# Attention denominators, row maxima and expert tokens turned as 32x32 squares on the vector engine instead of on the matrix engine

## The reference

```
xn  = layernorm(x)
q, k, v = xn @ Wq, xn @ Wk, xn @ Wv          # 16 heads of 64
attn = softmax(q @ k.T / 8)                   # per head, 2048 x 2048
a   = concat(attn @ v) @ Wo + bo
e   = argmax_e(xn @ router_w[e])              # 8 experts, one per token
f   = square(relu(xn @ expert_fc[e])) @ expert_proj[e].T
out = x + a + f
```

## Time and profile before

| | us |
|---|---|
| runs of the kernel | 1388.52 median of 3 (1387.92 to 1388.96) |
| the profiled execution, its own time | 1389.63 |
| its span, first to last instruction | 1387.9 |
| PE busy | 1365.8 (98% of the span) |
| POOL busy | 1121.8 (81%) |
| DVE busy | 1078.0 (78%) |
| ACT busy | 735.2 (53%) |
| the 16 DMA engines, the kernel's own transfers | 20.8% of their span |
| mean granted TensorE clock | 0.993 of full speed |

### The profile page before, as it was taken

One profiled execution on the slowest core, in us unless ns is written; L12 is line 12 of the kernel. 1 busy time (PEld: TensorE's weight loads), 2 busy tenths in 40 slices (PEclk: granted clock), 3 DMA queues, 4 the chain that ended last, 5 costly groups with the idle time before them and its releaser, 6 DMA issues.

```text
span 1387.9 us, 20006 instructions
## 1 busy us (share of the span) xinstructions
PE 1365.8 (98%) x6447; PEld 866.1 (62%) x6447; DVE 1078.0 (78%) x1468; ACT 735.2 (53%) x1316; POOL 1121.8 (81%) x908
## 2 busy tenths in 40 slices
PE   7899999999999999999999999999999999999997
PEld 4566666566665666666766666656667666656644
DVE  7987887786787767777777777778677777788877
ACT  4465455565464554554644645545546446556543
POOL 7779997777787877877878877879777788789995
PEclk8999999999999999999999999999999999999998
DMA  4241113220132201331113311123112231111000
GB/s 104 58 120 41 37 41 70 70 67 20 43 89 57 60 19 43 94 69 44 34 39 84 73 40 43 43 71 90 24 42 55 64 79 26 24 23 33 11 19 23
DMA packets 65255, 72.38 MB, mean 52 GB/s; under 512 B 9024, under 2 KB 38272, under 8 KB 65152
## 3 DMA queue, kind: packets, MB, share of 16 engines
q1 hardware_dynamic: 64128, 69.01, 20.3%
q0 software_dynamic: 1024, 2.10, 0.5%
HBM read 17.83 MB, written 5.11 MB: 17 GB/s over the span
## 4 chain that ended last, share of the span: by engine, by line
PE 93%; DVE 2%; POOL 1%; DMA 1%; issue 1%; SPq 1%; ACT 1%; POOLq 0%; DVEq 0%; ACTq 0%
PE OB L1116 31%; PE SB L1062 17%; PE SB L1069 16%; PE MB L1088 15%; PE XB L1153 2%; PE XB L1144 2%; PE XB L1162 2%; PE XB L1050 1%; PE XB L1043 1%; POOL acc L505 1%; DVE mx L767 1%; PE XB L1123 1%; PE XB L1125 1%; PE XB L1124 1%; DMA K<-low 1%
## 5 line engine op out<-in xcount | busy, mean ns | idle before, releaser
L505 POOL TENSOR_TENSOR acc<-acc,ex 128x512 f32<-128x512 f32 x717 | 915.9, 1304 | 99.9 <-DVE acc L790 40.4
L767 DVE TENSOR_REDUCE mx<-MB 128x1 f32<-128x512 f32 x992 | 655.9, 688 | 228.9 <-PE MB L1088 224.1
L619 ACT ACTIVATE ex<-SB 128x512 f32<-128x512 f32 x1024 | 607.2, 599 | 329.8 <-PE SB L1069 262.0
L1116 PE MATMUL OB<-ex,V 128*64 128x512 f32 x2048 | 452.7, 594 | 0.0
L1062 PE MATMUL SB<-Q,K 128*128 128x512 f32 x1024 | 421.9, 412 | 0.5 <-ACT ex L619 0.5
L1069 PE MATMUL SB<-Q,K 128*128 128x512 f32 x1024 | 399.8, 390 | 0.8 <-DMA Q<-mrow 0.8
L1088 PE MATMUL MB<-K,Q 128*128 128x512 f32 x992 | 389.1, 392 | 1.6 <-DVE mx L773 0.6
L1116 PEld LDWEIGHTS OB<-ex,V 128*64 128x64 f32 x2048 | 143.9, 137 | 284.3 <-issue 273.0
L1062 PEld LDWEIGHTS SB<-Q,K 128*128 128x128 f32 x1024 | 192.6, 188 | 96.5 <-issue 53.5
L790 DVE TENSOR_TENSOR acc<-acc,ex 128x512 f32<-128x512 f32 x179 | 205.0, 1145 | 13.5 <-ACT ex L619 1.0
L1088 PEld LDWEIGHTS MB<-K,Q 128*128 128x128 f32 x992 | 186.1, 188 | 46.7 <-DVE mx L767 5.0
(11 more groups left out here) (136 smaller groups left out, 608.8 us busy)
## 6 DMA issues: line engine op xcount, KB each, us to landing
Q<-high SPq DMA_DIRECT2D x124, 128.0 KB, 2.3
K<-high SPq DMA_DIRECT2D x112, 128.0 KB, 2.3
Q<-low SPq DMA_DIRECT2D x64, 128.0 KB, 2.4
K<-low SPq DMA_DIRECT2D x56, 128.0 KB, 2.3
w<-fc SPq DMA_DIRECT2D x23, 256.0 KB, 2.7
w<-projT SPq DMA_DIRECT2D x23, 256.0 KB, 3.1
sorted_x<-res SPq DMA_DIRECT2D x1, 1472.0 KB, 6.9
tok<-sorted_x SPq DMA_DIRECT2D x23, 64.0 KB, 1.7
```

The costliest lines, as they stand in the source:

```text
L505: pool.tensor_tensor(a[:, :], src[:, :], EX[h][ex_slot(kt)][:, :], ALU.add).then_inc(done, 1)
L619: act.activation(EX[h][ex_slot(kt)][:, :], SB[bank_of(n, 2 * kt + h)][:, :], ACT.Exp).then_inc(a_e[h], 1)
L767: dve.tensor_reduce(mx[:, m % 2, u:u + 1], MB[bank_of(m, i)][:, :], AX.X, ALU.max).then_inc(v_m, 1)
L1116: mm = pe.matmul(OB[own[h], :], V[(n // JB) % 2][:, k, own[h]], EX[h][ex_slot(k)][:, :], start=(k == 0), stop=(k == NT - 1))
```

## The change

It takes the three turns away from PE and gives them to DVE, whose transpose turns each 32x32 square of a tile by itself.

- **Denominators.** `denominators`, `take_sums` and `invert` are gone. At kt 0 of block n DVE runs `fold_sums(n - 1)`: for each head it transposes `acc` (128x512) into `rd` in squares and reduces the squares' rows, which leaves 16 columns; together a 128x32 tile `part`, in which the four groups of 32 partitions are still to be added. `sum_parts` does this in one small operation a step: kt 1 a copy of 64x32, kt 2 an add of 64x32, kt 3 a copy of 32x32, kt 4 an add of 32x32, kt 5 the reciprocal of 32x32, kt 6 a transpose of 32x32 into `row`. SP writes `row` to DRAM (`store_row`), waits for it, and reads it back spread over 64 partitions for each head (`spread_rd`) into `rd`. POOL's `normalise` stays at kt 10 and waits for these transfers.
- **Maxima.** `nm` has 32 columns, of which 8 are used; `turn_max` is four DVE transposes of 32x32 at kt 12 straight into `mrow`. The matmul and ACT's copy are gone.
- **Tokens.** The tile is read in four transfers that put the 32x32 squares in each other's place, and one DVE transpose of 128x128 at kt 3 finishes the turn. The matmul and ACT's copy are gone.

The last block's denominators are still made on PE.

```
-AT_DEN, AT_KV, AT_Q, AT_WO, AT_NM, AT_T = 8, (1, 9), 5, 13, 11, 12
-AT_INV, AT_ON = 8, 10
+AT_KV, AT_Q, AT_WO, AT_NM, AT_T = (1, 9), 5, 13, 11, 12
+AT_FOLD, AT_ON = 0, 10
...
+        turned = rd
+        spare = halves[:, :, :].rearrange("p t s -> p (t s)")
+        part, upper, half = (spare[0:r, k * SQ:(k + 1) * SQ] for k, r in enumerate((P, 2 * SQ, 2 * SQ)))
+        third, den, inv, row = (sb(n_, [SQ, SQ]) for n_ in ("third", "den", "inv", "row"))
+        rows_rd = nc.dram_tensor("rows_rd", (2, QB), F32, kind="Internal").ap()
...
+                def store_row(n):
+                    wait(sp, v_row, n.times(1, 1))
+                    wait(sp, d_rd, n.times(32))
+                    sp.dma_start(rows_rd.rearrange("h (t b) -> (h t) b", b=SQ), row[:, :]).then_inc(d_row, 16)
+
+                def spread_rd(n):
+                    wait(sp, d_row, n.times(16, 16))
+                    for h in range(2):
+                        sp.dma_start(rd[own[h], :], rows_rd[h:h + 1, :].to_broadcast([DH, QB])).then_inc(d_rd, 16)
...
                 def normalise(n):
-                    wait(pool, v_rd, n.times(2, 2))
-
+                    wait(pool, d_rd, n.times(32, 32))
                     wait(pool, a_o, n.times(1, 1))
...
+                def turn_max(m):
+                    wait(dve, v_nm, m.times(1, 1))
...
+                    for j in range(P // SQ):
+                        squares = slice(j * SQ, (j + 1) * SQ)
+                        ins = dve.transpose(mrow[:, squares].bitcast(F32), nm[squares, :].bitcast(F32))
+                    ins.then_inc(v_mrow, 1)
...
+                def turn_tokens(r):
+                    wait(dve, d_tile, r.times(TD, TD))
+                    wait(dve, t_up, r.times(1))
+                    dve.transpose(tokT[:, :], tok[:, :]).then_inc(v_tok, 1)
...
+                def fold_sums(n):
+                    for h in range(2):
+                        wait(dve, sums[h][n % 2], added(n, NT - 1))
+                        if h == 0:
+                            wait(dve, g_on, n.times(1))
+                        else:
+                            wait(dve, v_part, n.times(2, 1))
+                        dve.transpose(turned[:, :], acc[h][n % 2][:, :]).then_inc(v_turn, 1)
+                        wait(dve, v_turn, n.times(2, h + 1))
+                        dve.tensor_reduce(part[:, h * QB // SQ:(h + 1) * QB // SQ], turned[:, :].rearrange("p (t k) -> p t k", k=SQ),
+                                          AX.X, ALU.add).then_inc(v_part, 1)
+
+                def sum_parts(n, kt):
+                    if kt == 1:
+                        wait(dve, v_part, n.times(2, 2))
+                        dve.tensor_copy(upper[:, :], part[2 * SQ:4 * SQ, :]).then_inc(v_upper, 1)
+                    if kt == 2:
...
+                        dve.tensor_tensor(half[:, :], part[0:2 * SQ, :], upper[:, :], ALU.add).then_inc(v_sum2, 1)
...
+                    if kt == 6:
+                        wait(dve, v_inv, n.times(1, 1))
+                        wait(dve, d_row, n.times(16))
+                        dve.transpose(row[:, :], inv[:, :]).then_inc(v_row, 1)
```

More of the change, by code:

```diff
@@ L646, in kv @@
                                        ACT.Copy).then_inc(a_v, 1)
-                def max_rows(m):
-                    wait(act, t_nm, m.times(1, 1))
-                    if not (m.i is None and m.off == 0):
-                        old = m - 1
-                        wait(act, d_nm[old % QS], (old // QS).times(32, 32))
-                    act.activation(mrow[:, :], XB[0:2 * TB, 0:P], ACT.Copy).then_inc(a_nm, 1)
                 def take_o(n):
@@ L693, in high_q0 @@
                     ins.then_inc(a_q, 1)
-                def copy_tokens(r):
-                    wait(act, t_tok, r.times(1, 1))
-                    act.activation(tokT[:, :], XB[:, 0:P], ACT.Copy).then_inc(a_tok, 1)
                 def rectify(r):
@@ L753, in one @@
                             high_q(m)
-                        if kt == AT_DEN and not (n.i is None and n.off == 0):
-                            take_sums(n - 1)
-                        if kt == AT_T and before(n, NB - 1):
-                            max_rows(n + 1)
                 schedule(act, first, one, lambda: take_o(Lin(NB - 1)))
@@ L777, in minus_max @@
                     wait(dve, v_m, m.times(UNITS, UNITS))
-                    wait(dve, t_nm, m.times(1, -1))
-                    dve.tensor_reduce(nm[:, m % 2, :], mx[:, m % 2, :].rearrange("p (a b) -> p a b", b=JB), AX.X,
+                    if m.off == 0:
+                        dve.wait_ge(g_i, 6)
+                    dve.tensor_reduce(nm[:, 0:2 * TB], mx[:, m % 2, :].rearrange("p (a b) -> p a b", b=JB), AX.X,
                                       ALU.max, negate=True).then_inc(v_nm, 1)
+                def turn_max(m):
+                    wait(dve, v_nm, m.times(1, 1))
+                    if not (m.i is None and m.off == 0):
+                        old = m - 1
+                        wait(dve, d_nm[old % QS], (old // QS).times(MD, MD))
+                    for j in range(P // SQ):
+                        squares = slice(j * SQ, (j + 1) * SQ)
+                        ins = dve.transpose(mrow[:, squares].bitcast(F32), nm[squares, :].bitcast(F32))
+                    ins.then_inc(v_mrow, 1)
                 def add(n, kt):
@@ L936, in first @@
                         maxima(Lin(1), u)
+                        if u == 0:
+                            turn_max(Lin(0))
                     choose()
@@ L948, in one @@
                             minus_max(n + 1)
+                        if kt == AT_T and before(n, NB - 1):
+                            turn_max(n + 1)
                         if kt in AT_KV and before(n, NB - JB):
@@ L959, in one @@
                         add_own(n, kt)
-                        if kt == AT_INV and not start:
-                            invert(n - 1, 0)
-                            invert(n - 1, 1)
+                        if kt == AT_FOLD and not start:
+                            fold_sums(n - 1)
+                        if not start:
+                            sum_parts(n - 1, kt)
                         for part in AT_PLACE.get((n.off, kt), ()):
@@ L1146, in make_kv @@
                         mm.then_inc(t_v, 1)
-                def denominators(n):
-                    take_spare(a_den, n.times(1, 1))
-                    for h in range(2):
-                        wait(pe, sums[h][n % 2], added(n, NT - 1))
-                    for h in range(2):
-                        mm = pe.matmul(XB[own[h], :], ones[:, 0:DH], acc[h][n % 2][:, :], start=True, stop=True)
-                    mm.then_inc(t_den, 1)
                 def project(n):
@@ L1164, in project @@
                     mm.then_inc(t_wo, 1)
-                def turn_max(m):
-                    take_spare(a_nm, m.times(1, 1))
-                    wait(pe, v_nm, m.times(1, 1))
-                    pe.transpose(XB[0:2 * TB, 0:P], nm[:, m % 2, :], ident[:, :]).then_inc(t_nm, 1)
                 def first():
@@ L1206, in first @@
                             logits(c)
-                    for u in range(EARLY):
-                        max_unit(Lin(1), u)
-                    turn_max(Lin(0))
-                    for u in range(EARLY, MIDDLE):
+                    for u in range(MIDDLE):
                         max_unit(Lin(1), u)
@@ L1238, in one @@
                             project(n - 1)
-                        if kt == AT_T and before(n, NB - 1):
-                            turn_max(n + 1)
-                        if kt == AT_DEN and not start:
-                            denominators(n - 1)
                         for m, tile, tiles in batches(n, kt):
```

74 lines of the change are left out of this document (40 added, 34 removed).

## The result

The changed kernel takes **1466.61 us** (median of 4 runs, 1462.48 to 1470.92), the kernel before 1388.74 in the same comparison: a ratio of **1.054 (1.048 to 1.061)**. The forecast was 1393.8 in a range of 1374 to 1413: the sign was right, the size was not, and the range did not hold it.

The account below looks back on a forecast made before the run. PE was taken to bound the kernel, busy 98% of the span. 1389.6 - 28.5 + 4.7 + 1.4 + 22 + 0.7 + 5 = 1394.9 us, less 1.1 over the median: 1393.8 us, range 1374 to 1413 (the forecast's own 1385 to 1403).

Parts of the forecast that it names:

- the ledger: DVE's lateness at kt 1 to 6: PE stalls 0.6 us per V block, 1.15 per K block, +22 us in all.
- less 0.9 for the XB job of `expert_up`: kt 4: the add's lateness, 1.2 - 0.15, is cut by 0.9 us of DVE idle time, leaving a 0.1 us stall.
- PE's relief: Matmuls taken from PE: 0.91 us a block for denominators, 0.12 for maxima, 0.12 for tokens; 34.7 us at most.
- The fold at kt 0: Two transposes and two reductions on DVE, 2.9 us, fit in 3.46 us idle under the batch and cost nothing.
- The short operations wait until POOL's addition ends, reductions don't: kt 1 to 6: DVE's small copies and adds wait for POOL's running add; reductions keep their 0.69 us.
- second rival: kt 1 to 6: every small DVE operation just misses and waits a whole POOL add; 41 us, 1413 us; chance 0.22.
- A wait is at most one addition: kt 1 to 8: a small operation waits until POOL's 1.3 us add ends, 0.6 us for a chance arrival.
- The late POOL: POOL's late adds delay the fold: +4.7 us at block 3, +1.4 at 28 and 29; blocks 1 and 2 win nothing.
- The tail, +5: Block 31: the reciprocal and its transfers come late for POOL's normalising, +5 us (2 to 8).
- The first rival: kt 1 to 6: small operations slip past POOL; stalls 7 us, tail +1.7, 1375.5 us; chance 0.22.
- The signs: L948, L951, L954 average 0.7 us or more; PE's new `mx` waits 20; block 3 units at 176; last `normalise` waits 10.
- `turn_max` at nothing: kt 12: four DVE transposes, 0.44 or 0.76 us, against 0.7 us of room; zero in the sum.

Follow-up runs that it names:

- fold_last: The change with small copies and additions as one-source reductions, folds and all six small operations at kt 8 (last block: kt 0); 1370.87 us, ratio 0.986.
- sums_kt8: The change with all six small operations at kt 8, copies and two-source additions kept, fold still at kt 0; 1393.0 us, ratio 1.001.
- one_source: The change with its two small copies and two small additions written as one-source reductions, same places; 1387.57 us, ratio 1.000.
- tokens_pe: The change with the expert tokens turned by PE and copied by ACT as before; 1433.84 us, ratio 1.034.
- tok_kt0: The change with the tokens still turned on DVE, but at kt 0 behind the fold in place of kt 3; 1435.88 us, ratio 1.034.

## Why the prediction was wrong

The step that failed most is the ledger's kt 4: "less 0.9 for the XB job of `expert_up`". It took that job as time in which DVE catches up, while the job itself waits for DVE. This term alone comes to 28.4 us in blocks 4 to 27. Two more were sized wrong: the lock waits between the maxima, and the edges, where a wait outlasts one addition and the clock falls with it.

By columns, for the profiled execution: the forecast has +0.7 ahead of block 1, 0 for blocks 1 and 2, +4.3 for block 3, -6.5 for 4 to 27, +1.4 for 28 to 30 and +5 for the end. Measured are -1.9, +6.4, +7.5, +44.6, +18.1 and -1.8. So 51 us of the miss lie in 4 to 27 and 17 in 28 to 30. Step by step, as the prediction put them:

- **PE's relief** (1.15 us in a block with tokens): right in v blocks, 1.17 in fold_last. In k blocks it is 0.86; what takes the 0.3 there was not looked for. Over 4 to 27 fold_last has -24.0 where the step gives 24 x 1.03 + 23 x 0.12 = 27.5.
- **The fold at kt 0, at nothing**: right in the middle (sums_kt8), with 0.71 us for a transpose where 0.69 was taken.
- **The short operations wait until POOL's addition ends, reductions don't**: right, and shown by one_source. The lengths by step were not as the ledger had them: at kt 1 to 4 they are 0.31, 1.28, 1.21 and 1.03 us in a k block (1.3 and then two short waits in the ledger) and 0.35, 0.58, 1.22 and 1.03 in a v block. So in k blocks the prediction's hope of a "short phase" at kt 2 and 3 failed. Both operations arrive within 0.1 us after one of POOL's additions has begun. Timelines of block 9, DVE and then POOL:

```profile
451.12 1.28 DVE L951 TENSOR_TENSOR halves<-halves 64x32 f32<-64x32 f32 x1
452.33 1.27 DVE L773 TENSOR_REDUCE mx<-MB 128x1 f32<-128x512 f32 x2
453.63 1.21 DVE L954 COPY third<-halves 32x32 f32<-32x32 f32 x1
```

```profile
453.54 2.49 POOL L533 TENSOR_TENSOR acc<-acc,ex 128x512 f32<-128x512 f32 x2
```

  A wait ends where one addition of POOL meets the next; two reductions then take 1.27 and POOL's addition 1.25, so the next short operation just misses. That is the mechanism of the second rival, "in step against POOL": it holds for two of the four operations in every k block and for the one at kt 3 in v blocks, not for all four. Its 41 us for 25 blocks are near the 38 that own time and lock waits make over 4 to 27 (10.5 and 27.4, below), in part by luck, as one_source's own time holds a wait for the tokens.
- **"less 0.9 for the XB job of `expert_up`"** is the step that failed most. At kt 4, where the ledger has a stall of 0.1, this job was booked as time in which DVE catches up. But since the change the job itself waits for DVE, for the transposed tokens that stand behind the locked copy of kt 3. The wait comes to 38.4 us in 23 blocks, and taking it away (tokens_pe, tok_kt0) is worth some 30, 12.0 of them by the clock at 0.50 in six blocks. The prediction had counted the tokens' turn by its length on DVE only, and never asked who waits for its result.
- **The ledger as a whole**: 0.6 us for a v block and 1.15 for a k block (its items add up to 1.1). Measured as the change less fold_last: 0.67 + 1.17 = 1.84, and 2.16 + 0.86 = 3.02. The runs split it, v and k: short operations' own time 0.43 and 0.78 (one_source less sums_kt8; 0.2 and 0.4 in the prediction), lock waits 0.69 and 1.49 (tok_kt0 less one_source), tokens behind the lock 0.71 and 0.70 (the change less tok_kt0), and 2.3 to 3.6 in blocks 4, 8, 9, 16, 20 and 21, where the clock falls too. Over blocks 4 to 27 the same differences are 10.5, 27.4 and 28.4 us, and with 2.3 between sums_kt8 and fold_last the lateness comes to 44.6 + 24.0 = 69 us where 22 stood.
- **A wait is at most one addition**: wrong. Six waits outlast it: 2.48 in block 1, 2.28 and 2.47 in block 2, 3.71 in block 3, and 4.68 and 4.67 in blocks 29 and 30. A term for PE's clock after a stall was missing altogether: 3.0 us in block 29, 12.0 in the six blocks of the middle.
- **The late POOL**: +4.7 in block 3, with blocks 1 and 2 at nothing, and +1.4 for 28 and 29. Measured +7.5 for block 3 and +6.4 for 1 and 2, and +18.1 for blocks 28 to 30. The place was right, the price was taken from one addition. In block 3 POOL's last addition ended at 177.68 and not at 173.48, and `find_owners` held DVE for 4.2 us where 1.5 stood, so the units began at 183.27 and not at 176.
- **The tail, +5**: wrong, -1.8 with the end. DVE's row goes out at 1434.43 and POOL normalises at 1439.99 (5.6 us, of which 4.6 were forecast for the transfers), but POOL waits only 0.95 us: its own additions are slow beside DVE's, 2.1 us each (14.93 for 7), and end late. The cover was not gone.
- **The first rival** (nothing waits for POOL, 1375.5) is what one_source makes true, at 1387.57. In the profiled execution it stands at -3.5 where the rival's terms give -12.6. Block 3 has 4.5 us more than they say, and blocks 4 to 27 have 9.1 more: 3.3 of own time (10.5 where 7.2 stood) and 5.8 of PE's relief (21.7 in sums_kt8 where 27.5 stood). Ahead of block 1 and at the end it is 5.3 less.
- **The signs**: the copies and additions average 0.71, 0.91 and 1.14 us (0.7 or more forecast) and the long transpose 0.71 (0.69), both as foretold. PE's new waits for `mx` come to 39.6 us, and PEld's to 60.4, where some 20 stood, and POOL's last `normalise` waits 0.95 us where 10 stood.
- **`turn_max` at nothing**: right. The four take 0.83 us together, near the upper of the two values (0.76): each begins 0.01 us after the one ahead has ended, and the room covers it. This agrees with the Trainium skill's rule on a change of quadrant (VectorE: DVE Perf Modes, section "Two Vector instructions with no wait between them"); four transposes in one quadrant stand in no run, so that the quadrant is the cause is not shown.

**Still open**: what decides whether DVE gets in between two of POOL's additions. In the middle every waiting operation gets in at the next boundary. The six long waits above let one to three boundaries go by, and each ends in POOL's first pause, as in block 2:

```profile
137.75 1.29 POOL L533 TENSOR_TENSOR acc<-acc,ex 128x512 f32<-128x512 f32 x1
...
140.40 1.27 POOL L533 TENSOR_TENSOR acc<-acc,ex 128x512 f32<-128x512 f32 x1
```

L951 arrives there at 137.84 and ends at 140.31, after two additions, in the gap ahead of 140.40. Lengths and distances of POOL's additions are the same in both cases (1.25 to 1.30 us). No run was made to tell more. Open as well is why the clock falls in six K blocks and not in the other six.

## What to carry to other kernels

Before an operation is moved onto DVE, ask three things: does its form wait for POOL, who waits for its result and stands that result behind such a wait, and is DVE idle at the place where it is put. A small copy or addition on SBUF can be written as a one-source reduction, and then runs in its 0.2 us beside a busy POOL. Time may be booked as slack only if the job that gives it does not itself depend on the engine that is late. Price a stall of PE of some us with the slower matmuls behind it.
